# Norms and transposes of the first MoE layer, moved from stages of their own into the attention program before it

## What is computed

```python
x = layernorm(x + causal_attention(x))              # 16 heads of 16
x = layernorm(x + cross_attention(x, ctx_768))      # 1024 keys for each of 4 sequences
def rmsnorm(x, gamma):
    n = norm(x, axis=-1, keepdims=True)
    return x / maximum(n, 1e-12) * 16 * gamma
xn = rmsnorm(x, norm_gamma)                         # 2048 rows
sn = rmsnorm(slot_embeds, slot_norm_gamma)          # 8 experts x 128 slots
logits = einsum('bnd,esd->bnes', xn, sn)            # then two softmaxes, experts, and so on
```

## Time and profile before

| what | value |
|---|---|
| median of 3 runs | 2954.07 us (2953.14 to 2954.84) |
| the profiled execution | 2954.8 us, span 2953.1 us |
| PE, DVE, ACT, POOL busy | 86%, 51%, 45%, 15% of the span |
| mean granted TensorE clock | 0.933 of full |
| last group's drain (ACT L1364) | starts 786.34 us |
| last layer norm of the program applied (POOL L1156) | 801.32 to 806.16 us |
| fetch of the embeddings issued (SP L172) | 809.21 us |
| first matmul of the routing stage (PE L1740) | 859.73 us |

### The profile page before, as it was taken

One profiled execution on the slowest core, in us unless ns is written; L12 is line 12 of the kernel. 1 busy time (PEld: TensorE's weight loads), 2 busy tenths in 40 slices (PEclk: granted clock), 3 DMA queues, 4 the chain that ended last, 5 costly groups with the idle time before them and its releaser, 6 DMA issues. The chain is left out here.

```text
span 2953.1 us, 47417 instructions
## 1 busy us (share of the span) xinstructions
PE 2536.9 (86%) x15793; PEld 1452.1 (49%) x15794; DVE 1502.1 (51%) x4196; ACT 1340.6 (45%) x2886; POOL 456.4 (15%) x719
## 2 busy tenths in 40 slices
PE   6999999999549889997889899898977995399991
PEld 3555544444224456675555544343434654267761
DVE  2555877888044500024544588777735663222224
ACT  3655467766444422111445457565664552022220
POOL 4233211110200000000122212212023001400004
PEclk8999999999969999998899999999998996599996
DMA  6544533321000022114633433232322325501113
GB/s 207 165 138 139 132 87 93 75 59 43 6 12 1 1 91 91 60 47 151 182 105 122 133 97 90 58 92 63 78 68 75 108 66 189 176 31 32 32 32 91
DMA packets 153825, 259.89 MB, mean 88 GB/s; under 512 B 22712, under 2 KB 96704, under 8 KB 149440
## 3 DMA queue, kind: packets, MB, share of 16 engines
q1 hardware_dynamic: 150544, 248.81, 28.8%
q0 software_dynamic: 3072, 8.39, 0.9%
HBM read 180.71 MB, written 81.53 MB: 89 GB/s over the span
## 5 line engine op out<-in xcount | busy, mean ns | idle before, releaser
L1357 ACT ACTIVATE second_p<-psum 128x512 f32<-128x512 f32 (+3 forms) x1024 | 461.9, 522 | 278.9 <-PE psum L1223 275.4
L1357 ACT ACTIVATE first_p<-psum 128x512 f32<-128x512 f32 (+3 forms) x768 | 365.8, 548 | 171.5 <-PE psum L1223 168.5
L1431 DVE TENSOR_REDUCE second_max_parts<-psum 128x1 f32<-128x512 f32 x512 | 321.5, 682 | 67.7 <-PE psum L1200 66.5
L1431 DVE TENSOR_REDUCE first_max_parts<-psum 128x1 f32<-128x512 f32 x512 | 322.2, 682 | 57.4 <-PE psum L1200 55.6
L1427 DVE CUSTOM_DVE_ANT_0 second_masked<-psum,mask_qk 128x384 f32<-128x384 f32 (+3 forms) x512 | 229.2, 488 | 194.5 <-PE psum L1200 169.8
L1213 PE MATMUL psum<-second_q,second_k 64*128 64x512 f32 (+3 forms) x1024 | 226.1, 437 | 42.8 <-DVE second_max_parts L1431 27.1
L1235 PE MATMUL psum<-second_p,second_v_aug 128*32 128x512 f32 (+3 forms) x2048 | 238.6, 538 | 8.4 <-ACT second_p L1357 8.1
L1200 PE MATMUL psum<-second_k,second_q 64*128 64x512 f32 (+3 forms) x1024 | 201.9, 391 | 27.9 <-DMA second_k<-a_k_parts 15.6
L1213 PEld LDWEIGHTS psum<-second_q,second_k 64*128 64x128 f32 x1024 | 98.1, 187 | 231.3 <-issue 84.0
L1223 PE MATMUL psum<-second_shift_T,choose 64*128 64x512 f32 (+3 forms) x1024 | 197.6, 381 | 0.0
L1235 PE MATMUL psum<-first_p,first_v_aug 128*32 128x512 f32 (+3 forms) x1536 | 184.1, 551 | 11.6 <-ACT first_p L1357 11.6
(11 more groups left out here) (317 smaller groups left out, 3800.4 us busy)
## 6 DMA issues: line engine op xcount, KB each, us to landing
first_k<-c_k_parts SPq DMA_DIRECT2D x64, 256.0 KB, 4.7
second_q<-a_q_parts SPq DMA_DIRECT2D x128, 128.0 KB, 2.9
second_k<-a_k_parts SPq DMA_DIRECT2D x128, 128.0 KB, 2.9
second_k<-c_k_parts SPq DMA_DIRECT2D x64, 256.0 KB, 4.6
first_q<-a_q_parts SPq DMA_DIRECT2D x64, 128.0 KB, 2.9
first_k<-a_k_parts SPq DMA_DIRECT2D x64, 128.0 KB, 2.9
c_k_parts<-first_held SPq DMA_DIRECT2D x16, 512.0 KB, 3.1
first_q<-c_q_parts SPq DMA_DIRECT2D x64, 128.0 KB, 4.5
```

What stands on the lines that cost most here:

```text
L1357: evacuated(act.activation(probs[tile % 2][:, 2 * h + p, q0:SEQ], bank[:, q0:SEQ], ACT.Exp, scale=scale), event)
L1431: evacuated(v.reduce_max(max_parts[n % 2][:, h, p, qt, k0 // BANK:k0 // BANK + 1], bank[:, 0:width], axis=AX_X), event)
```

## The change

The norm and the transposes of the slots, and the norm and transposes of the rows, become pieces of the attention program. New kinds: `slot_stats`, `slot_root`, `slot_rows`, four `slot_turn`; and for each context slot `rms_rows` and two `rms_turn`. `slot_stats` and `slot_root` are added behind the front pieces of group 19; `slot_rows` and the turns make up group 20, behind a `rest` of cost 3000 that places nothing; the rows of slots 4, 5 and 6 are in groups 22, 26 and 30, also behind a rest, where the output pieces of these slots are in groups 21, 25 and 29; those of slot 7 stand behind its output pieces at the end. The mean square is taken from the batch-norm statistics: mean squared plus variance for the slots; for rows after the layer norm it follows from the variance alone. The roots are Newton steps on POOL, in one pass of 8 columns for the layer norm and the row scale. For the last slot alone, DVE makes the two bases, ACT takes their roots with its Sqrt, DVE inverts them and applies norm and scale row by row, and the transposes wait for row by row. The embeddings and the two gains are fetched by SP at the start of the attention program, after the first layer's weights. The context's transposed copies lie in the storage that later holds `slot_T` and `xT`. Nine semaphores are new; the first stage had 35, the row norm stage has 20. The rest of the kernel is unchanged.

```diff
-S_KINDS = ("scores", "shift", "oturn", "xturn", "split", "value")
+S_KINDS = ("scores", "shift", "oturn", "xturn", "split", "value", "slot_turn", "rms_turn")
...
+def slot_pieces():
+    return [("slot_rows", 0, 0)] + [("slot_turn", 0, u) for u in range(EXPERTS // QT * DK)]
+def rms_pieces(slot):
+    return [("rms_rows", slot, 0)] + [("rms_turn", slot, k) for k in range(DK)]
...
-COST = {"oturn": 450, "xturn": 450, "oproj": 1750, "split": 1750, "value": 1750}
+REST = ("rest", 0, 0)
+COST = {"rest": 3000, "rms_turn": 450, "oturn": 450, "xturn": 450, "oproj": 1750, "split": 1750, "value": 1750}
...
-            plan.append(stream.pop(0)[0])
+            event = stream.pop(0)[0]
+            if event != REST:
+                plan.append(event)
...
-        near = sb("near", [P, 3, QT])
+        near, two_roots = sb("near", [P, 3, 2 * QT]), sb("two_roots", [P, 2 * QT])
+        if soft:
+            rms_scale, rms_gain, slot_gain = sb("rms_scale", [P, QT]), sb("rms_gain", [P, D]), sb("slot_gain", [P, D])
+            slot_stats, slot_mean_var = sb("slot_stats", [P, EXPERTS, 6]), sb("slot_mean_var", [P, EXPERTS, 2])
+            slot_root = sb("slot_root", [P, EXPERTS])
+            last_base, last_root, last_scale = sb("last_base", [P, 2, QT]), sb("last_root", [P, 2, QT]), sb("last_scale", [P, 2, QT])
+            last_based, last_rooted, last_ready = sem("last_based"), sem("last_rooted"), sem("last_ready")
+            soft_in, slot_done, slot_inverted, slot_ready = sem("soft_in"), sem("slot_done"), sem("slot_inverted"), sem("slot_ready")
+            scaled, spread = sem("rms_scaled"), sem("rms_rows")
...
-            ctx_T = [sb(f"ctx_T{i}", [P, 2, CTX_SEQ]) for i in range(2)]
+            if soft:
+                ctx_T = [soft["slot_T"], soft["xT"][:, :, 0:CTX_SEQ]]
+            else:
+                ctx_T = [sb(f"ctx_T{i}", [P, 2, CTX_SEQ]) for i in range(2)]
...
+        applied_late = len(slots) - 1 if slots[-1].scaled else None
...
+                if soft:
+                    embeds = soft["rows"][:, 0:EXPERTS, :]
+                    sp.dma_start(embeds, a["L0_ffn_slot_embeds"].rearrange("e s d -> s e d")).then_inc(soft_in, 16)
+                    sp.dma_start(slot_gain[:, :], a["L0_ffn_slot_norm_gamma"].partition_broadcast(P)).then_inc(soft_in, 16)
+                    sp.dma_start(rms_gain[:, :], a["L0_ffn_norm_gamma"].partition_broadcast(P)).then_inc(soft_in, 16)
...
+                def roots_with_scale(slot):
+                    variance, place = mean_var[:, :, 1], scale_at[slot]
+                    step(pool.tensor_scalar(near[:, 0, 0:QT], variance, LN_EPS, None, ALU.add))
+                    step(pool.tensor_scalar(near[:, 0, QT:2 * QT], variance, ROW_LEAST, None, ALU.max))
+                    newton(two_roots[:, :], 2 * QT)
+                    step(pool.tensor_copy(rstd[:, :], two_roots[:, 0:QT]))
+                    wait_for(pool, spread, QT * place)
+                    step(pool.tensor_tensor(near[:, 2, 0:QT], two_roots[:, QT:2 * QT], near[:, 0, 0:QT], ALU.mult))
+                    pool.tensor_tensor(rms_scale[:, :], near[:, 2, 0:QT], rstd[:, :], ALU.mult).then_inc(scaled, 1)
...
+                    if slot == applied_late:
+                        return
                     pool.wait_ge(aggregated, QT * (done + 1))
-                    root_of(mean_var[:, :, 1], rstd)
+                    if slots[slot].scaled:
+                        roots_with_scale(slot)
+                    else:
+                        root_of(mean_var[:, :, 1], rstd)
...
+                def root_slots():
+                    pool.wait_ge(slot_done, 2 * EXPERTS + 2)
+                    step(pool.tensor_scalar(near[:, 0, 0:EXPERTS], slot_root[:, :], SLOT_LEAST, None, ALU.max))
+                    newton(slot_root[:, :], EXPERTS, slot_inverted)
...
+                def slot_turn(event):
+                    u = event[2]
+                    pe.wait_ge(slot_ready, EXPERTS)
+                    wait_bank(pe, event)
+                    bank = bank_of(event)
+                    for q in range(QT):
+                        ins = pe.transpose(bank[:, q * P:(q + 1) * P],
+                                           soft["rows"][:, u // DK * QT + q, u % DK * P:(u % DK + 1) * P], c.ident[:, :])
+                    filled(ins, event)
+                def rms_turn(event):
+                    _, slot, k = event
+                    wait_bank(pe, event)
+                    bank = bank_of(event)
+                    for q in range(QT):
+                        pe.wait_ge(spread, QT * scale_at[slot] + q + 1)
+                        ins = pe.transpose(bank[:, q * P:(q + 1) * P],
+                                           soft["rows"][:, slot % BATCH * QT + q, k * P:(k + 1) * P], c.ident[:, :])
                     filled(ins, event)
...
+                def slot_turned(event):
+                    u = event[2]
+                    bank = wait_full(act, event)
+                    evacuated(act.activation(soft["slot_T"][:, u % DK, u // DK * SEQ:(u // DK + 1) * SEQ], bank, ACT.Copy), event)
+                def rms_turned(event):
+                    _, slot, k = event
+                    bank = wait_full(act, event)
+                    b = slot % BATCH
+                    evacuated(act.activation(soft["xT"][:, k, b * SEQ:(b + 1) * SEQ], bank, ACT.Copy), event)
...
+                    elif kind == "slot_turn":
+                        slot_turned(event)
+                    elif kind == "rms_turn":
+                        rms_turned(event)
+                    elif kind == "apply" and event[1] == applied_late:
+                        act.wait_ge(last_based, 2)
...
+                def measure_slots():
+                    v.wait_ge(soft_in, 48)
+                    for e in range(EXPERTS):
+                        v.bn_stats(slot_stats[:, e, :], soft["rows"][:, e, :]).then_inc(slot_done, 1)
+                    v.wait_ge(slot_done, EXPERTS)
+                    for e in range(EXPERTS):
+                        v.bn_aggr(slot_mean_var[:, e, :], slot_stats[:, e, :]).then_inc(slot_done, 1)
+                    v.wait_ge(slot_done, 2 * EXPERTS)
+                    v.tensor_tensor(slot_root[:, :], slot_mean_var[:, :, 0], slot_mean_var[:, :, 0], ALU.mult).then_inc(slot_done, 1)
+                    v.wait_ge(slot_done, 2 * EXPERTS + 1)
+                    v.tensor_tensor(slot_root[:, :], slot_root[:, :], slot_mean_var[:, :, 1], ALU.add).then_inc(slot_done, 1)
+                def scale_slots():
+                    v.wait_ge(slot_inverted, 1)
+                    for e in range(EXPERTS):
+                        v.scalar_tensor_tensor(soft["rows"][:, e, :], soft["rows"][:, e, :], slot_root[:, e:e + 1], slot_gain[:, :],
+                                               ALU.mult, ALU.mult).then_inc(slot_ready, 1)
+                def rms_row(slot, t, scale):
+                    v.scalar_tensor_tensor(soft["rows"][:, slot % BATCH * QT + t, :], x_of(slot)[:, t, :], scale[:, t:t + 1],
+                                           rms_gain[:, :], ALU.mult, ALU.mult).then_inc(spread, 1)
+                def rms_rows(slot):
+                    place = scale_at[slot]
+                    if slot == applied_late:
+                        v.wait_ge(last_rooted, 1)
+                        v.reciprocal(last_root[:, :, :], last_root[:, :, :]).then_inc(last_ready, 1)
+                        v.wait_ge(last_ready, 1)
+                        v.tensor_tensor(last_scale[:, 0, :], last_root[:, 1, :], last_base[:, 0, :], ALU.mult).then_inc(last_ready, 1)
+                        v.wait_ge(last_ready, 2)
+                        v.tensor_tensor(last_scale[:, 1, :], last_scale[:, 0, :], last_root[:, 0, :], ALU.mult).then_inc(last_ready, 1)
+                        for t in range(QT):
+                            v.tensor_scalar(x_of(slot)[:, t, :], x_of(slot)[:, t, :], mean_var[:, t, 0:1], last_root[:, 0, t:t + 1],
+                                            ALU.subtract, ALU.mult).then_inc(applied, 1)
+                            v.wait_ge(applied, QT * norm_at[slot] + t + 1)
+                            if t == 0:
+                                v.wait_ge(last_ready, 3)
+                            rms_row(slot, t, last_scale[:, 1, :])
+                        return
+                    v.wait_ge(scaled, place + 1)
+                    if place == 0:
+                        wait_full(v, ("slot_turn", 0, EXPERTS // QT * DK - 1))
+                    v.wait_ge(applied, QT * (norm_at[slot] + 1))
+                    for t in range(QT):
+                        rms_row(slot, t, rms_scale)
...
+                    elif kind == "slot_stats":
+                        measure_slots()
+                    elif kind == "slot_rows":
+                        scale_slots()
+                    elif kind == "rms_rows":
+                        rms_rows(event[1])
+                    elif kind == "apply" and event[1] == applied_late:
```

(29 more changed lines are left out.)

43 lines of the change are left out of this document (27 added, 16 removed).

## The result

The changed kernel takes 2921.42 us (median of 4 runs, 2916.28 to 2923.57) against 2953.61 for the kernel before in the same session: ratio 0.9888, 95% interval 0.9874 to 0.9903. The time is inside the range of 2905 to 2925, 5.7 us above the forecast of 2915.7; the gain is 32.2 us, where 38.4 were forecast. The profiled execution took 2920.47 us (span 2918.72), 34.4 us of span less than the profiled one of before. In later sessions the kernel before had single runs of 3006 and 8651 us at a lower granted clock (0.89 and 0.46), which stand in no ratio here.

A forecast was written before the change was run, and what follows sets the result against it. PE bounds most of the kernel, but 796.85 to 859.73 us is a serial chain no matmul covers. Removed stages −52.2, PE work +4.2 and +0.2, stalls +9.4 sum to −38.4: 2915.7 us, range 2905 to 2925.

The forecast's parts named there:

- The removed stages: Fetch, slot norm and row norm stages after attention go; routing matmul at 807.55 in place of 859.73: 52.2 us gained.
- Scale and gain: At the attention program's new end, per row a scale, a wait and a gain product: 0.87 us, four times.
- The table load: Loading ScalarE's root table at the attention's end takes 1.28 us but starts before the root is needed: costs nothing.
- rival 4: Attention's end doesn't shorten as said (table load or stage end): 1.3 to 4 us less gain, 2917 to 2920; chance 0.06.
- TensorE's turns: Transposes moved into attention groups, 0.52 us each: 2.1 in group 20, 1.04 each in 22 and 26; group 30 nearly free.
- Stalls in group 20: PE waits behind VectorE's blocks: 3.2 us for slot statistics, 4.6 at the first slot turn behind the slot rows.
- rival 1: Stalls in the attention groups are absorbed as queues refill: −45.8, 2908.3 us; chance 0.2.
- The rows in groups 22 and 26: Four gain products on VectorE delay the score maxima: PE stalls 0.8 us in each group, bounds 0 and 1.7.
- The granted clock: No clock fall charged at group 20's stalls; full clock had lasted 4.5 us after PE's last matmul; low routing start unchanged.
- rival 2: Attention stalls at the upper bound, 12.5 us, plus one or two clock falls at 2.2 each: −30.9, 2923.2 us; chance 0.22.
- The added DMAs: Three more SP issues at the attention's start, 1.25 MB, fill an idle stretch: nothing, bounds 0 and 1.5 us.
- The text's own tests: Wrong if groups 19 and 20 cost under 5 or over 14 us more, clock falls there, or earlier parts move over 1.5.

The follow-up runs named there:

- E2: Changed kernel with the eight slot statistics spread singly between group 16's turns, aggregation and root behind group 17's pieces; 2915.12 us, ratio 0.9865.
- E3: E2 plus the eight slot rows in pairs between group 18's turns, leaving group 20 only the slot's transposes with their copies; 2913.81 us, ratio 0.9863.
- E1: Changed kernel with the three added transfers issued behind SyncE's load of group 11 instead of at the start; 2918.38 us, ratio 0.9877.
- E9: Changed kernel with group 20's block of eight slot rows issued as four pairs, the rest kept ahead of them; 2918.28 us, ratio 0.9869.
- E8: Changed kernel with group 20's block of eight slot rows issued as four pairs, without the rest; 2918.07 us, ratio 0.9871.
- E6: E3 plus E1's late fetch, slot rows starting one turn later in group 18, last two in group 19; 2909.98 us, ratio 0.9839; repeat 2907.89, 0.9836.

## Why the prediction was right or wrong

- **The removed stages**: forecast −52.2, measured −52.2 from the last drain to the first of the next program, and 10.5 us from aggregate to routing matmul where 10.7 were said. Scale and gain took 0.85 a row for 0.87, the stage end 3.97 for 3.75. The table load was hidden, as said; rival 4 falls.
- **TensorE's turns**: 1.7 us in group 20 for 2.1, 1.05 in each of groups 22 and 26 for 1.04, 0.1 in group 30.
- **Stalls in group 20**: 2.84 for 3.2 and 4.54 for 4.6. E2 and E3 show each to be the block's own: with its cause moved, each goes whole. The stalls were not absorbed: rival 1 falls.
- **The rows in groups 22 and 26**: forecast 0.8 each, measured nothing beyond the turns (group 22's 26.03 is 24.98 + 1.05). Four gain products delay the maxima and TensorE waits 0.6, but it had that idle anyway.
- **The granted clock**: forecast to stay, measured two falls in group 20 at 1.6 each. The sum took the row that showed the full clock for 4.5 us after the last matmul as cover for a stall of 2.84 with 4.54 behind it. The step that failed is that a wait under 4.5 us was counted as safe. The row was one reading and no safe length: at the end of the changed kernel the clock falls 3.4 us after TensorE's last product (813.74 to 817.14), in E2 2.6 us into its wait, and E3's wait of 2.65 us was enough. Of rival 2 this half came true, its longer stalls did not; its 2923.2 is nearer to the median than the forecast. The Trainium skill, TensorE: Matmul & The Clock Gate, Part 1, has the throttled state as the default, which activity releases; the rows at 487 and 507 us, at 0.50 behind the two waits, agree. The routing stage starts low as forecast, and the clock rises 4.6 us into it (830.79).
- **The added DMAs**: "they fill an idle stretch: nothing, bounds 0 and 1.5". Measured 3.3 at the first drain of this profile and 2.3 on average, outside the bounds, and given back by E1. The argument looked at SyncE's queue between two issues, where it was indeed idle. The transfers issued before it were still under way on the DMA engines, and the first product waits for the last of them. In this profile this was the largest term that was wrong; by the mean of 2.3 the clock in group 20, 3.1, is larger.
- **The text's own tests**: groups 19 and 20 cost 12.2 more, inside 5 to 14; but the clock fell there, and something before 440 us moved by more than 1.5. By these the forecast's mechanism is wrong in two places, though the time is inside the range. Part of that nearness is luck: 8.1 us of costs that were not forecast stand against 4.1 us the other way. From profile to profile, the 4.0 us between −38.4 and −34.4 are: start-up +3.3, clock in group 20 +3.1, group 9's fall +1.7, the rows of groups 22 and 26 −1.6, waits and turns in group 20 −0.8 (7.38 for 7.8 and 1.7 for 2.1), the other groups together −0.7, and −1.0 behind the change.

## What to carry to other kernels

When work is slipped between the pieces of a full engine, the price is the size of the block in the queue it goes through, not its sum: eight rows of 0.41 us cost 6.8 us as one block, with the clock's share, and nothing spaced out over two groups; in four pairs within half a group they still cost about 1.2 us of waits (E9). A spaced piece must come after its own input is ready, or its engine's queue passes the wait on to everyone behind it. And a fetch "in an idle stretch" has to be checked against transfers in flight that the first work waits for, not against the queue that issues it.

## What the runs showed of the hardware that was not expected

The granted clock fell for 3.4 us behind a wait of 2.84 us of an engine that was 99% busy in the group before (28.41 of 28.79 us). Of the seven profiles with that wait, six have the fall 1.2 to 1.4 us behind it, and E8 has none. It also fell in one or two of the groups 5 to 14 in ten of the fourteen profiles: in group 9 in six of them, the kernel before among them, in 5, 11, or 13 and 14 in the others, though no edit touches what the engines compute in these groups. Ten of these eleven falls stand within 0.7 us of the end of a wait of 1.27 to 2.01 us (before the output projections of groups 5, 9 and 13, and for keys at the end of group 10); the other, in E8's group 14, stands behind two of 0.5 and 0.6. All fourteen profiles have these waits, and most times the clock stays up. Where the instructions are the same, profiles differ by some us: in the second program the time at the low clock goes from 88.7 to 102.4 us, and the first to the last drain takes 1029.2 to 1034.3 us, mostly longer where more of it is at the low clock. Such differences can hide a gain made upstream, as in E6 and E9. Why one execution has such a fall behind a wait and the next has none is open. In the profiles it went with a first stretch of 23.9 us at the low clock instead of 20.5, save in E8, which had 20.5 and two falls; nothing here sets it on purpose. Whether E9's long stretch hangs on its edit was not tried.
